# Layer 1's causal attention regrouped: four heads and half of the queries per unit, two heads per maximum, four heads' values together

## The chip, the cores and the metric

The kernel runs on one core of a Trainium2 chip. The metric is the device time of one execution in microseconds (us). A core has five engines that run their own instruction streams in order and meet at semaphores: PE (TensorE, matmuls; PEld is its weight load), DVE (VectorE), ACT (ScalarE), POOL (GpSimd) and SP (SyncE, which here only issues DMAs). Matmul results land in PSUM, eight banks of 128 partitions x 512 f32.

## The reference, cut to what matters

Two transformer layers on 1024 tokens of 256 values, each with attention, a mixture of experts, and a modulated layer norm ahead of each. The change is in layer 1's attention alone. There, 16 heads of 16 values attend causally, with a linear bias per head on the key's position (ALiBi):

```python
q = h @ Wq + bq; k = h @ Wk + bk; v = h @ Wv + bv        # h: 1024 x 256, 16 heads of 16
s = (q_h @ k_h.T) / 4 + slope_h * (key - query)          # key <= query only
o_h = softmax(s) @ v_h
x = x + gate * (concat(o_h) @ Wo + bo)
```

## The kernel before

**What a head's work is.** Queries and keys are cut into bf16 parts that are stacked on the contraction axis (`qst`, `kst`: 107 rows), so one bf16 matmul gives scores of f32 quality. For one head and one half of the queries (512 of 1024) the kernel makes:

- maxima: scores with queries on the partitions, per block of 128 queries (`j` 0 to 3) and 512 keys (`kh`), as wide as the causal mask leaves them (128, 256, 384 or 512 keys), a mask matmul on the diagonal block, and a DVE reduction to one maximum per query (`pe_max16`, `dve_max16`, L1216 to L1226);
- the row: the negated maxima go as two bf16 parts into rows 99 to 106 of `qst`, so that the next scores come out with the maximum taken off: three small DVE operations (`dve_neg`), a PE transpose into bank 6 (`pe_tr`, L1004) and a DVE product with a 0/1 mask over 11 x 512 (`dve_row16`, L1008);
- score tiles: the transposed scores, 128 keys x up to 512 queries (`pe_st16`, L1242, mask L1245), exponentiated by ACT into `Pb` (`act_exp16`, L1258);
- values: `vx` (16 values and a column of ones per head) against `Pb`, an f32 matmul with 17 output rows. Four key blocks of one head go to four 32-row strips of one bank (4 or 5), side by side (`pe_pv16`, L1279);
- the end: ACT copies the bank to `OTa` (`act_ot16`, L1291), four f32 matmuls with `esum` add the strips and transpose (`pe_evac16`, L1299), DVE divides by the sum and writes `octx` (`dve_evac16`, L1308, L1310).

**Tiling and order.** A unit is one head and one half: 32 units, head by head, the halves in turn. The first half has 4 key blocks, the second 8. `causal_order` writes one list that all engines follow; maxima run two units ahead of the score tiles. Maxima rotate over banks 0, 1 and 7, score tiles over banks 2 and 3, `Pb` over 9 buffers. `OTa` has one buffer per half.

**The stacks.** SP writes projected parts to DRAM (`sp_scratch`) and loads them back stacked (`sp_stack`), in three groups: heads 0 to 3, 4 to 7 and 8 to 15 (`GROUPS`), each group's loads behind the one before on one queue. `pe_max16` waits for the group of its head on `stacked[g]`.

**Layer 0's stage of the same shape.** Layer 0's pattern attention (`pattern_order`) already runs units of four heads and half of the queries: `pe_maxp` makes two heads' scores into a pair of banks ("slot", two slots: banks 0 and 1, 2 and 3), `dve_maxp` reduces both at once (L1074, 1024 values), `pe_shift` with `mc` and `act_shift` bring the maxima to `qst2`, score tiles rotate over banks 4, 5 and 7, `pe_pvp` puts four heads in the four strips of bank 6, `pe_evacp` does four heads at once through a slot (L1166). It has no causal mask, and its stacks have 64 rows, so two heads' score matmuls can run on PE together.

Of the kernel before, what the change touches and what calls it, by code (L numbers as in the profile page):

```python
# [15 lines left out]
H = 16  # L16
# [9 lines left out]
GROUP_OF = [0] * 4 + [1] * 4 + [2] * 8  # L26
# [7 lines left out]
LOADS2 = (((0, 0, 2), (48, 0, 1)), ((0, 0, 2), (48, 1, 1)))  # L34

# [10 lines left out]
def max_steps(nh, half, causal):  # L46

    out = []
    for a in range(nh):
        for j in range(4):  # L50
            keys = (4 * half + j + 1) * 128 if causal else T
            for kh in range(2):
                c = min(512, keys - 512 * kh)
                if c > 0:
                    out.append((a, j, kh, c))
    return out


def attention_order(nu, nh, causal, group, ahead, lag, at_begin, at_step, evac, lead=True):

    order, due, n = [], [], 0

    def steps_of(u):
        return [("max", u, *s) for s in max_steps(nh, u % 2, causal)]
# [11 lines left out]
    if lead:  # L76
        order += steps_of(0)
    neg, row = unit_head(0)
    order += neg + row
    if ahead == 2:  # L80
        order += steps_of(1)
    for u in range(nu):
        nk = (4 * (u % 2) + 4 if causal else NT) * nh
        todo = steps_of(u + ahead) if u + ahead < nu else []
        total, given = len(todo), 0
        begin, last_max = (0, nk) if ahead == 2 else (3 * (u % 2), nk - 5)
        order += at_begin(u)
        ready = []
        for k in range(nk):
# [7 lines left out]
            if ahead == 1:  # L97
                for _ in range(due_now // 2):
                    order.append(todo.pop(0))
                    due_now -= 1  # L100
# [8 lines left out]
            if len(ready) == group * nh:  # L109
# [14 lines left out]
def main_order():  # L124
# [19 lines left out]
    order = attention_order(16, 2, False, 2, 1, (2, 3, -4, -2), at_begin, at_step, evac, lead=False)  # L144
# [5 lines left out]
def pattern_order():  # L150
# [27 lines left out]
    first = [("mmax", *s) for s in max_steps(2, 0, False)]  # L178
# [59 lines left out]
def program(nc, a, out):  # L238
# [42 lines left out]
    esum = sb("esum", [128, 17], F32)  # L281
# [144 lines left out]
    octx = sb("octx", [128, NT, D], F32, at=F.at)  # L426
# [102 lines left out]
    def dve_stats(e, n, half):  # L529
        hs = slice(4 * half, 4 * half + 4)  # L530
        for j in range(4):
            i = 4 * half + j
            if n < 2:
                if j == 0 and n == 0:
                    e.wait_ge(d_x[half], 16)
                elif j == 0:
                    e.wait_ge(b6_ok[2], B6M["project", 14 + half, 1] + 1)
                e.bn_stats(st6[:, i, :], x[:, i, :]).then_inc(st_ok, 1)
# [180 lines left out]
    def sp_rows(e, l, g):  # L719
        hs = slice(*GROUPS[g])  # L720
        for st, n in ((qst, "qrow"), (kst, f"krow{l}")):
# [201 lines left out]
    NO_M, NO_C = numbered(MAIN), numbered(CAUSAL)  # L923
# [24 lines left out]
    def last_max(order):  # L948

        out, n = {}, 0  # L950
        for s in order:
            if s[0] == "max":
                n += 1
                out[s[1]] = n
        return out

# [10 lines left out]
    def bank6_table(order, kinds):  # L967

        out, n = {}, 0
        for s in order:  # L970
# [5 lines left out]


    mx_mm, mp_ok, neg_ok, tr_mm, b6_ok, st_mm, exp_ok, pv_mm, ot_ok, neg_v = (
        [s, s, sem(f"{n}m")] for n, s in ((n, sem(f"{n}16")) for n in (
            "mx_mm", "mp_ok", "neg_ok", "tr_mm", "b6_ok", "st_mm", "exp_ok", "pv_mm", "ot_ok", "neg_v")))  # L980
    ev_mm, ev_v, clear_ok, mcat_one = ([s, s] for s in (sem(n) for n in ("ev_mm", "ev_v", "clear_ok", "mcat_one")))
    ST_MM0 = EXP_OK0 = (0, 256, 0)
    NEG_OK0, OT_OK0, PV_MM0, EV_V0 = (0, 16, 0), (0, 8, 0), (0, 64, 0), (0, 16, 0)
    CLEAR_OK0 = (0, 1, 0)

    def dve_neg(e, i, u, nh, two, last):

        dst, low = mcat[:, u % 2, 0:nh, 3:7], mcat[:, u % 2, 0:nh, 7:11]
        e.wait_ge(mp_ok[i], last)
        if two:  # L990
            e.tensor_reduce(dst, mp[:, u % 3, 0:nh, :, :], AX, ALU.max, negate=True).then_inc(neg_v[i], 1)
        else:
            e.tensor_scalar(dst, mp[:, u % 3, 0:nh, :, 0], -1.0, None, ALU.mult).then_inc(neg_v[i], 1)
        e.wait_ge(neg_v[i], 2 * u + 1)
        e.tensor_copy(mbf[:, 0:nh, :], dst).then_inc(neg_v[i], 1)
        e.wait_ge(neg_v[i], 2 * u + 2)
        e.tensor_tensor(low, dst, mbf[:, 0:nh, :], ALU.subtract).then_inc(neg_ok[i], 1)

    def pe_tr(e, i, u, nh, before):
        e.wait_ge(neg_ok[i], NEG_OK0[i] + u + 1)  # L1000
        if before:
            e.wait_ge(b6_ok[i], before)
        for h in range(nh):
            last = e.transpose(bank[6][0:11, 128 * h:128 * h + 128], mcat[:, u % 2, h, :], idf[:])  # L1004
        last.then_inc(tr_mm[i], 1)
# [15 lines left out]
    RING, TILEP, BANK_P0, SHIFT = {}, {}, {}, {}  # L1021
    ring_free, slot_, turn_ = [None, None], 1, 0
    tile_free = {4: (lat_ok, LAT_ALL), 5: (lat_ok, LAT_ALL), 7: (fold_ok, 6)}
    for s_ in PATTERN:
        if s_[0] in ("max", "evac"):
            slot_ = 1 if s_[0] == "evac" and s_[1] >= 6 else 1 - slot_
            RING[s_] = (len(RING), slot_, ring_free[slot_])
            ring_free[slot_] = (ring_ok, len(RING))
        elif s_[0] == "shift" and s_[1] < 2:
            slot_ = 1 - slot_  # L1030
            SHIFT[s_[1]] = (2 * slot_, ring_free[slot_])
            ring_free[slot_] = (sh_ok, s_[1] + 1)
        elif s_[0] in ("shift", "st"):
            for a_ in range(2 if s_[0] == "st" else 1):
                b_ = (4, 5, 7)[turn_ % 3]
                turn_ += 1
                if s_[0] == "st":
                    TILEP[s_[1:] + (a_,)] = (len(TILEP), b_, tile_free[b_])
                    tile_free[b_] = (exp_ok[0], len(TILEP))
                else:  # L1040
                    SHIFT[s_[1]] = (b_, tile_free[b_])
                    tile_free[b_] = (sh_ok, s_[1] + 1)
        elif s_[0] == "product" and s_[2] == 0:
            b_ = (4, 5, 7)[turn_ % 3]
            turn_ += 1
            BANK_P0[s_[1]] = (b_, tile_free[b_])
            tile_free[b_] = (pc_ok, s_[1] + 1)
    NPBP = 11

    def pe_ring(e, s):  # L1050

        _, slot, free = RING[s]
# [4 lines left out]
    def pe_maxp(e, s):  # L1057
        _, w, j, kh = s
        hp, qi = w // 4 * 2 + w % 2, w // 2 % 2 * 4 + j
# [3 lines left out]
        slot = pe_ring(e, s)  # L1063
        for a in range(2):
            r = slice(64 * a, 64 * a + 64)
            last = e.matmul(wide[slot][:, a, :], qst2[r, hp, qi * 128:qi * 128 + 128], kst2[r, hp, cols(kh)],  # L1066
                            start=True, stop=True)
        last.then_inc(ring_mm, 1)

    def dve_maxp(e, s):  # L1070
        _, w, j, kh = s
        r, slot, _ = RING[s]
# [3 lines left out]
    def dve_negp(e, w):  # L1076

        n, m = nm[:, w % 2, :].rearrange("p (a j) -> p j a", a=2), mc[w % 2][:].rearrange("p j (a c) -> p j a c", a=2)
        e.wait_ge(ring_ok, RING["max", w, 3, 1][0] + 1)
        e.tensor_reduce(nm[:, w % 2, :].rearrange("p (a j) -> p a j", a=2), mp[:, w % 3, :, :, :], AX, ALU.max,  # L1080
# [70 lines left out]
    def act_otp(e, s):  # L1151
        _, u, kt = s
        if kt != NT - 1:
            return
# [1766 lines left out]
```

## Time and profile before

| | us |
|---|---|
| median of 3 runs | 1561.76 (1561.07 to 1561.95) |
| the profiled execution | 1559.81, of it span 1558.0 |

| engine | busy us | share |
|---|---|---|
| PE | 1423.2 | 91% |
| DVE | 924.2 | 59% |
| ACT | 746.3 | 48% |
| POOL | 548.4 | 35% |

The stage that the change touches runs from 1160.5 us (its first score matmul) to 1349.3 us (the first matmul of the output projection), 188.8 us or 12% of the span. Matmul records overlap: a record's own length is longer than the step from its start to the next one's, so PE's cost is read from the distance of starts, not from the sum of lengths. A f32 matmul leaves two records ("x8" is four matmuls).

### The profile page before, as it was taken

Reading aid. Unit: us, or ns where it says so; the run is one execution under the profiler, and the core shown is the slowest. Engines: PE = TensorE matmul, PEld = TensorE weight load, DVE = VectorE, ACT = ScalarE, POOL = GpSimd, SP = SyncE. Lnnn points to the kernel's source line nnn. Section 1 sums busy time; section 2 is a strip of 40 time slices with the busy share of each in tenths; the row PEclk is TensorE's granted clock in tenths of the full one; section 3 lists DMA queues with packets and bytes.
Section 4 is the critical chain, followed back from the end, with each engine's and each line's share of the span. In section 5 each row is a group of like instructions: output and inputs, shape, how many; then the busy total and the mean of one; then the engine's idle time right before and its main releaser. Section 6 shows DMA issues by size and latency. Waiting matters only on the chain. (4 is left out here: it accounts for less than half of the span.)

```text
span 1558.0 us, 20601 instructions
## 1 busy us (share of the span) xinstructions
PE 1423.2 (91%) x7350; PEld 837.9 (54%) x7350; DVE 924.2 (59%) x1719; ACT 746.3 (48%) x1368; POOL 548.4 (35%) x454
## 2 busy tenths in 40 slices
PE   6889999899999999999999968899689999779998
PEld 3533333355555545454555546788544444468887
DVE  5598776356566666666666343444458787534445
ACT  3468776654445454545454334233135555435553
POOL 4260152055565656556565531233300000101210
PEclk9999999999999999999999978899789999959999
DMA  7660000000000000000001011111064000101110
GB/s 291 162 135 1 6 16 8 1 1 0 1 1 0 1 1 1 1 1 1 1 1 42 1 40 36 41 41 41 1 181 81 1 1 1 51 21 41 43 40 28
DMA packets 19050, 53.03 MB, mean 34 GB/s; under 512 B 4198, under 2 KB 7032, under 8 KB 17667
## 3 DMA queue, kind: packets, MB, share of 16 engines
q1 hardware_dynamic: 18949, 51.72, 11.7%
q8 instruction: 59, 0.97, 0.3%
q14 instruction: 42, 0.34, 0.1%
HBM read 42.28 MB, written 8.39 MB: 33 GB/s over the span
## 5 line engine op out<-in xcount | busy, mean ns | idle before, releaser
L1643 POOL TENSOR_TENSOR Ps<-Ps,Pb 128x512 f32<-128x512 f32 x192 | 245.2, 1292 | 161.5 <-ACT Pb L1626 161.5
L1626 ACT ACTIVATE Pb<-bank 128x512 f32<-128x512 f32 x256 | 152.7, 597 | 288.2 <-PE bank L1615 287.7
L1587 DVE TENSOR_REDUCE mp<-bank 128x1 f32<-128x512 f32 x256 | 171.6, 686 | 143.4 <-PE bank L1580 141.4
L1074 DVE TENSOR_REDUCE mp<-bank 128x2 f32<-128x1024 f32 x128 | 153.1, 1221 | 45.4 <-PE bank L1066 45.2
L1133 ACT ACTIVATE Pb<-bank 128x512 f32<-128x512 f32 x256 | 133.3, 601 | 40.6 <-PE bank L1116 40.2
L1580 PE MATMUL bank<-qk1h,qk0h 128*128 128x512 f32 x256 | 136.0, 543 | 7.6 <-DVE mp L1587 7.6
L1612 PE MATMUL bank<-qk0h,qk1h 128*128 128x512 f32 x256 | 124.3, 486 | 6.1 <-DVE mrow L1008 6.1
L1657 PE MATMUL bank<-Pb,kvx 128*64 128x512 f32 x512 | 124.0, 605 | 0.7 <-ACT Pb L1626 0.7
L1258 ACT ACTIVATE Pb<-bank 128x512 f32<-128x512 f32 x192 | 84.7, 489 | 78.1 <-PE bank L1245 55.3
L1226 DVE TENSOR_REDUCE mp<-bank 128x1 f32<-128x512 f32 (+1 forms) x192 | 97.5, 550 | 13.7 <-PE bank L1216 11.5
L1614 PE MATMUL bank<-qk0h,qk1l 128*128 128x512 f32 x256 | 101.3, 396 | 0.0
L1613 PE MATMUL bank<-qk0l,qk1h 128*128 128x512 f32 x256 | 101.0, 394 | 0.0
L1615 PE MATMUL bank<-mrow,onesr 128*128 128x512 bf16 x256 | 100.1, 391 | 0.0
L1116 PE MATMUL bank<-qstr,kstr 64*128 64x512 f32 x256 | 87.9, 488 | 6.8 <-ACT Pb L1133 6.6
L2019 POOL TENSOR_TENSOR hl<-hf,hh 128x512 fp32r<-128x512 f32 x32 | 41.3, 1290 | 143.2 <-ACT hh L2006 143.2
L1822 POOL TENSOR_TENSOR cTt<-cTt,gab 128x256 f32<-128x256 f32 x8 | 6.5, 810 | 229.0 <-DVE cTt L1812 229.0
L1116 PEld LDWEIGHTS bank<-qstr,kstr 64*128 64x128 f32 x256 | 36.0, 185 | 86.3 <-ACT Pb L1133 58.2
L2286 POOL TENSOR_TENSOR v1l<-wr,v1h 128x512 fp32r<-128x512 f32 x25 | 32.0, 1282 | 140.6 <-ACT v1h L2281 140.6
L1643 POOL TENSOR_TENSOR Ps<-Pb,Pb 128x512 f32<-128x512 f32 x32 | 40.6, 1281 | 115.2 <-ACT Pb L1626 115.1
L1612 PEld LDWEIGHTS bank<-qk0h,qk1h 128*128 128x128 f32 x256 | 48.5, 189 | 53.7 <-issue 33.6
L1580 PEld LDWEIGHTS bank<-qk1h,qk0h 128*128 128x128 f32 x256 | 50.0, 195 | 47.6 <-DVE mp L1587 25.0
L1721 DVE SCALAR_TENSOR_TENSOR x<-bank,rcp,x 128x256 f32<-128x256 f32 x128 | 53.0, 476 | 33.1 <-PE bank L1706 33.1
(341 smaller groups left out, 3280.3 us busy)
## 6 DMA issues: line engine op xcount, KB each, us to landing
wr<-wf SPq DMA_DIRECT2D x25, 256.0 KB, 2.6
wraw<-wf SPq DMA_DIRECT2D x8, 768.0 KB, 4.1
scratch<-stgr SPq DMA_DIRECT2D x4, 1024.0 KB, 4.0
scratch<-stg SPq DMA_DIRECT2D x4, 768.0 KB, 6.2
owT<-owT SPq DMA_DIRECT2D x1, 2048.0 KB, 9.8
qbn<-qbn SPq DMA_DIRECT2D x1, 1536.0 KB, 14.9
qstr<-scratch SPq DMA_DIRECT2D x6, 256.0 KB
kstr<-scratch SPq DMA_DIRECT2D x6, 256.0 KB
```

The costliest lines, as they stand in the source:

```text
L1074: e.tensor_reduce(mp[:, w % 3, :, j, kh], wide[slot][:], AX, ALU.max).then_inc(ring_ok, 1)
L1116: e.matmul(bank[b][:], kst2[r, hp, kt * 128:kt * 128 + 128], qst2[r, hp, cols(u % 2)], start=True, stop=True).then_inc(st_mm[0], 1)
L1133: e.activation(Pbp[n % NPBP][:], bank[b][:], ACT.Exp, scale=0.25).then_inc(exp_ok[0], 1)
L1580: e.matmul(bank[b][:, 0:c], qh[:, qi * 128:(qi + 1) * 128], kh_[:, kh * 512:kh * 512 + c], start=True, stop=True).then_inc(mx_mm[2], 1)
L1587: e.tensor_reduce(mp[:, u % 3, hd, j, kh:kh + 1], bank[b][:, 0:c], AX, ALU.max).then_inc(mp_ok[2], 1)
L1612: e.matmul(o, kh[:, ks], qh[:, qs], start=True, stop=False)
L1613: e.matmul(o, kh[:, ks], ql[:, qs], start=False, stop=False)
L1614: e.matmul(o, kl[:, ks], qh[:, qs], start=False, stop=False)
L1615: e.matmul(o, onesr[:], mrow[u % 2 * 2 + hd][:], start=False, stop=True).then_inc(st_mm[2], 1)
L1626: e.activation(Pbm[n % NPBM][:], bank[b][:], ACT.Exp, scale=SC0).then_inc(exp_ok[2], 1)
L1643: e.tensor_tensor(Ps[z][:], first, Pbm[n % NPBM][:], ALU.add).then_inc(sum_ok, 1)
L1657: last = e.matmul(bank[b][64 * hd:64 * hd + 64, :], kvx[:, kt, :], Pbm[n % NPBM][:], start=(kt < 1), stop=(kt == NT - 1), skip_group_check ...
```

## The change

- **Units** are four heads (a quad) and one half: 8 units. The order is now half by half: units 0 to 3 are the first half of quads 0 to 3, units 4 to 7 the second half.
- **Maxima** are made for two heads into a slot of two banks (`pe_maxc`) and reduced together (`dve_maxc`): 96 reductions where there were 192. Widths and masks stay. The score matmuls are the same in number and width, still one head each.
- **The row** is replaced by layer 0's way: `dve_negc` (four small DVE operations per unit), `pe_shift` (four matmuls with `mc`, through one of banks 4, 5, 7 or a slot), and `act_shiftc`: two ACT copies per unit, 11 rows x 2 heads x 512. A 0/1 pattern in `kst` (`krow`) picks each head's rows. DVE's masked product is gone.
- **Score tiles** rotate over banks 4, 5 and 7 and over 18 `Pb` buffers.
- **Values** of four heads and the same key block stand in the four strips of bank 6; two key blocks are done in one go (`pe_pvp` with l = 1).
- **The end** is per unit of four heads: one copy of bank 6, one set of four matmuls, a reciprocal and a product: 8 where there were 32.
- Waits for the stacks stay on `stacked[g]`, now asked for in the order quad 0 (group 0), quad 1 (group 1), quad 2 and 3 (group 2), within the first half's units. What SP issues, and in which order, stays (but for one small constant less at the start, `esum`).
- POOL clears and presets `mc` for layer 1 (`pool_mc(e, 1)`).

```diff
+def pair_half(l, w):
+    quad, half = (w // 4, w // 2 % 2) if l == 0 else (w // 2 % 4, w // 8)
+    return 2 * quad + w % 2, half
...
 def causal_order():
-    def at_step(u, k):
-        return [("clear",)] if (u, k) == (0, 0) else []
-    return attention_order(32, 1, True, 4, 2, (2, 2, 0, 2), lambda u: [], at_step, lambda u: [(0, [("evac", u)])])
+    lead, steps = 12, [(2 * u, pr, kt) for u in range(8) for kt in range(pair_keys(1, 2 * u)) for pr in range(2)]
+    maxima = [("max", w, j, kh) for w in range(16) for j, kh in pair_max(1, w)]
+    order, behind, done = [], [], 0
+    def one_max():
+        order.append(maxima.pop(0))
+        w, n = order[-1][1], len(pair_max(1, order[-1][1]))
+        left = sum(m[1] == w for m in maxima)
+        if left == 0 and w % 2:
+            order.append(("neg", w // 2))
+        if left == n - 2 and w and w % 2 == 0:
+            order.append(("shift", w // 2 - 1))
+    for n in range(lead):
+        one_max()
+        done += 1
+    for s, (w, pr, kt) in enumerate(steps):
+        order.append(("st", w // 2, pr, kt))
+        if s == 1:
+            order.append(("clear",))
+        while maxima and done < lead + s + 1 + min(s, 32) // 4:
+            one_max()
+            done += 1
+            if not maxima:
+                order.append(("shift", 7))
+        if pr == 1 and kt % 2:
+            behind.append((s + 3, ("pv", w // 2, kt)))
+            if kt == pair_keys(1, w) - 1:
+                behind.append((s + 6, ("evac", w // 2)))
+        order.extend(b[1] for b in behind if b[0] == s)
...
+    def pe_maxc(e, s):
+        _, w, j, kh = s
+        hp, half = pair_half(1, w)
+        q0, k0, c = 512 * half + 128 * j, 512 * kh, 512 if kh < half else 128 * j + 128
+        if (j, kh) == (0, 0):
+            e.wait_ge(stacked[min(hp // 2, 2)], STACKED2 + STACKED)
+        slot = pe_ring(e, 1, s)
+        for a in range(2):
+            h = 2 * hp + a
+            last = e.matmul(wide[slot][:, a, 0:c], qst[0:99, h, q0:q0 + 128], kst[0:99, h, k0:k0 + c], start=True, stop=True)
+        if kh == half:
+            for a in range(2):
+                last = e.matmul(wide[slot][:, a, c - 128:c], idb[:], maskq[:], start=False, stop=True, skip_group_check=True)
+        last.then_inc(ring_mm, 1)
...
+        e.tensor_reduce(mpc[:, w // 2 % 3, a0:a0 + 2, j, kh], wide[slot][:, :, 0:c], AX, ALU.max).then_inc(ring_ok, 1)
...
+        for pr in range(2):
+            h = 2 * (hp + pr)
+            e.activation(qst[96:107, h:h + 2, cols(half)], bank[b][96:107, :].unsqueeze(1).to_broadcast([11, 2, 512]),
+                         ACT.Copy).then_inc(sh_ok, 1)
...
+        for t in kts:
+            c = tile_queries(l, half, t)[1]
+            for a in range(4):
+                hp = pair_half(l, 2 * u + a // 2)[0]
+                h, i = 2 * hp + a % 2, TILEP[l][u, a // 2, t, a % 2][0] - TILE0[l]
+                last = e.matmul(bank[6][32 * a:32 * a + 17, 512 - c:512], vx[:, t, h * 17:h * 17 + 17],
+                                PBR[l][i % len(PBR[l])][:, 0:c],
+                                start=(t == 0), stop=(t == pair_keys(l, 2 * u) - 1), skip_group_check=True)
```

In this order a step is one `("st", ...)`: the two score tiles of two heads for one key block. There are 96 steps, 8 per unit in the first half and 16 in the second. Twelve maxima come ahead of the first step, then 1.25 per step up to step 32 and one per step up to step 75; steps 76 to 95 have none.

## Rows read from the trace of the kernel before

**Rows 1.** Windows of the stage: engines' busy us (instructions), granted clock, DMA share, GB/s.
```profile
1160.50:1170.50 10.00, 7.67 (x38) 3.58 (x38) 8.83 (x24) 1.75 (x4) 0.00 (x0) 0.66 1.10 211
...
1160.50:1349.30 188.80, 175.32 (x1313) 88.13 (x1314) 145.43 (x387) 100.61 (x224) 0.00 (x0) 0.98 0.14 28
```
**Rows 2.** Groups by form, 1160.5 to 1349.3: busy us, mean ns of one | idle before.
```profile
L1226 DVE TENSOR_REDUCE mp<-bank 128x1 f32<-128x512 f32 x96 | 64.5, 685 | 12.9 <-PE bank L1216 11.5
...
L1279 PE MATMUL bank<-Pb,vx 128*17 128x512 f32 x192 | 49.9, 598 | 0.5 <-ACT Pb L1258 0.5
...
L1008 DVE TENSOR_TENSOR qst<-bank,dmask 11x512 bf16<-11x512 f32 x32 | 21.9, 684 | 9.2 <-PE bank L1004 7.2
...
L1242 PEld LDWEIGHTS bank<-qst,kst 107*128 107x128 bf16 x192 | 21.3, 111 | 48.2 <-ACT Pb L1258 39.3 <-issue 4.4 <-DVE qst L1008 1.2
...
L1291 ACT ACTIVATE OTa<-bank 128x512 f32<-128x512 f32 x32 | 19.1, 597 | 16.4 <-PE bank L1279 16.3
...
L1226 DVE TENSOR_REDUCE mp<-bank 128x1 f32<-128x256 f32 x32 | 13.2, 411 | 0.0
...
L1279 PE MATMUL bank<-Pb,vx 128*17 128x128 f32 x64 | 12.6, 278 | 0.0
...
L995 DVE CAST mbf<-mcat 128x4 bf16<-128x4 f32 x32 | 5.4, 170 | 1.1
```
**Rows 3.** Timeline of PE inside the stage: start us, length us.
```profile
1229.97 0.38 PE L1216 MATMUL bank<-kst,qst 99*128 99x512 bf16 x1
1230.19 0.38 PE L1242 MATMUL bank<-qst,kst 107*128 107x512 bf16 x1
...
1231.00 1.23 PE L1299 MATMUL bank<-esum,OTa 32*128 32x17 f32 x8 [0.26 <-DVE qst L1008]
1232.08 0.38 PE L1242 MATMUL bank<-qst,kst 107*128 107x512 bf16 x1
...
1233.11 1.05 PE L1279 MATMUL bank<-Pb,vx 128*17 128x512 f32 x8
1234.09 0.28 PE L1242 MATMUL bank<-qst,kst 107*128 107x256 bf16 x1
```
**Rows 4.** Timeline of layer 0's stage of four heads, same columns.
```profile
235.63 1.05 PE L1147 MATMUL bank<-Pb,vx 128*17 128x512 f32 x8
...
238.46 1.05 PE L1147 MATMUL bank<-Pb,vx 128*17 128x512 f32 x8
...
240.10 0.66 PE L1097 MATMUL bank<-idr,mc 128*128 128x128 f32 x4
```
**Rows 5.** Reductions of 1024 values in layer 0: ns min/median/max, first and last start.
```profile
L1074 DVE TENSOR_REDUCE mp<-bank x128: 1159/1225/1229, 54.5 to 266.6; 128x2 f32<-128x1024 f32 x128
```
**Rows 6.** ACT on 1024 columns, elsewhere in the kernel, same columns.
```profile
L1950 ACT ACTIVATE wh<-wraw x8: 1040/1048/1048, 910.0 to 1077.2; 128x1024 fp32r<-128x1024 f32 x8
```
**Rows 7.** Timeline: SP's issues of the third group's stacks, ACT's back-to-back tiles.
```profile
1161.46 1.25 SPq L732 DMA_DIRECT2D qst<-scratch  x3
1162.75 1.81 SPq L732 DMA_DIRECT2D kst<-scratch  x4
...
1171.76 1.08 ACT L1258 ACTIVATE Pb<-bank 128x512 f32<-128x512 f32 x2 [1.31 <-PE bank L1242]
```
**Rows 8.** Windows of the loads' end, columns as in Rows 1.
```profile
1168.00:1187.70 19.70, 17.99 (x129) 9.40 (x127) 16.52 (x45) 10.79 (x24) 0.00 (x0) 0.94 0.85 163
1187.70:1195.00 7.30, 7.05 (x62) 3.48 (x64) 6.01 (x17) 4.00 (x11) 0.00 (x0) 1.00 0.00 1
```
**Rows 9.** Layer 0's stage near its end, without maxima: timeline.
```profile
298.46 1.05 PE L1147 MATMUL bank<-Pb,vx 128*17 128x512 f32 x8
...
301.05 1.05 PE L1147 MATMUL bank<-Pb,vx 128*17 128x512 f32 x8
```
**Rows 10.** Window of that end, columns as in Rows 1.
```profile
270.00:304.00 34.00, 32.91 (x166) 10.99 (x169) 11.84 (x19) 23.84 (x46) 6.07 (x6) 0.96 0.00 1
```
**Rows 11.** All of layer 0's stage: its score tiles' first and last start.
```profile
L1116 PE MATMUL bank<-qstr,kstr x256: 383/496/793, 88.2 to 302.0; 64*128 64x512 f32 x128
```

More of the change, by code:

```diff
@@ L43, in numbered, with max_steps, attention_order @@
     return number
[L46 to L61, printed above, removed]
+def max_steps():
+    return [(a, j, kh, 512) for a in range(2) for j in range(4) for kh in range(2)]
+def attention_order(lag, at_begin, at_step, evac):
+    order, due, n, nu, nh, nk = [], [], 0, 16, 2, 2 * NT
     def steps_of(u):
-        return [("max", u, *s) for s in max_steps(nh, u % 2, causal)]
+        return [("max", u, *s) for s in max_steps()]
     def run_due():
@@ L96, in attention_order @@
             given += due_now
[L97 to L100, printed above, removed]
+            for _ in range(due_now // 2):
+                order.append(todo.pop(0))
+                due_now -= 1
             order.append(("st", u, a, kt))
@@ L720, in sp_rows @@
         hs = slice(*GROUPS[g])
-        for st, n in ((qst, "qrow"), (kst, f"krow{l}")):
+        for st, n in ((qst, "qrow"), (kst, "krow")):
             e.dma_start(st[96:107, hs, :], a[n][:, hs, :]).then_inc(stacked[g], 16)
@@ L984, in program @@
[L984 to L997, printed above, removed]
@@ L1001, in pe_tr @@
+    def pe_tr(e, u, before):
+        e.wait_ge(neg_ok[1], u + 1)
         if before:
-            e.wait_ge(b6_ok[i], before)
-        for h in range(nh):
+            e.wait_ge(b6_ok, before)
+        for h in range(2):
             last = e.transpose(bank[6][0:11, 128 * h:128 * h + 128], mcat[:, u % 2, h, :], idf[:])
-        last.then_inc(tr_mm[i], 1)
+        last.then_inc(tr_mm, 1)
     def masked_row(e, o, h):
@@ L1020, in program @@
         "ring_mm", "ring_ok", "sh_mm", "sh_ok", "nm_ok", "mc_ok", "pc_ok", "d_sw", "half_ok"))
[L1021 to L1034, printed above, removed]
+    mh_ok = sem("mh_ok")
@@ new lines, in act_shiftc, with pe_stc @@
+    def act_shiftc(e, u):
+        b, _ = SHIFT[1][u]
+        hp, half = pair_half(1, 2 * u)
+        e.wait_ge(sh_mm, 16 + u + 1)
+        for pr in range(2):
+            h = 2 * (hp + pr)
+            e.activation(qst[96:107, h:h + 2, cols(half)], bank[b][96:107, :].unsqueeze(1).to_broadcast([11, 2, 512]),
+                         ACT.Copy).then_inc(sh_ok, 1)
+    def pe_stc(e, s):
+        _, u, pr, kt = s
+        hp, half = pair_half(1, 2 * u + pr)
+        q0, c = tile_queries(1, half, kt)
+        if kt == 0:
+            e.wait_ge(sh_ok, 16 + 2 * u + pr + 1)
+        for a in range(2):
+            _, b, free = TILEP[1][u, pr, kt, a]
+            h = 2 * hp + a
+            e.wait_ge(*free)
+            last = e.matmul(bank[b][:, 0:c], kst[0:107, h, kt * 128:kt * 128 + 128], qst[0:107, h, q0:q0 + c],
+                            start=True, stop=True)
+            if kt >= 4 * half:
+                last = e.matmul(bank[b][:, 0:128], idb[:], maskk[:], start=False, stop=True, skip_group_check=True)
+            last.then_inc(st_mm[0], 1)
@@ L1140, in pe_pvp @@
             else:
[L1141 to L1148 removed]
+                e.wait_ge(clear_ok, l + 1)
@@ L1283, in act_ot16 @@
-    def act_ot16(e, s):
-        _, u, ready = s
-        half = u % 2
-        if ready[-1][1] != 4 * half + 3:
-            return
-        e.wait_ge(pv_mm[1], PV_MM0[1] + NO_C[s])
-        if u >= 2:
-            e.wait_ge(ev_mm[1], u - 1)
-        e.activation(OTa[half][:], bank[4 + half][:], ACT.Copy).then_inc(ot_ok[1], 1)
-    def pe_evac16(e, u):
-        half = u % 2
-        e.wait_ge(ot_ok[1], OT_OK0[1] + u + 1)
-        e.wait_ge(b6_ok[1], B6C["evac", u])
-        for j in range(4):
-            rows = 32 * (j + 1) if half == 0 else 128
-            last = e.matmul(bank[6][:, 128 + 17 * j:145 + 17 * j], OTa[half][0:rows, 128 * j:128 * j + 128],
-                            esum[0:rows, :], start=True, stop=True)
-        last.then_inc(ev_mm[1], 1)
```

514 lines of the change are left out of this document (242 added, 272 removed).

## The prediction

> **What bounds the kernel now.** I read the page first: PE is busy 91% of the span, no other engine above 59%. Then the windows. The stage that changes takes 188.8 us; in it PE's records cover 175 us, DVE's 145 and ACT's 101, at nearly full granted clock, 2.4 GHz, but for the first 10 us [rows 1]. So PE's queue sets this stage too. Last, the stage's groups and timeline, for what PE's time is made of. Records overlap, so I count the distance of starts: 0.22 us for a score matmul of 512 columns (so about 0.055 per 128), 0.98 us for four value matmuls of 512 to 128 columns side by side, 1.08 us for the four matmuls that end a unit [rows 3]. A mask matmul of 128 columns I take at 0.06 us. Four matmuls in four strips run together: that is why 0.98 and not a sum stands there.
>
> PE's sum before: maxima 73,728 columns and 128 masks, 31.4 + 7.7 = 39.1 us; score tiles the same, 39.1; values 48 groups of four at 0.97, 46.6; ends 32 x 1.0 = 32; transposes 32 x 0.11 = 3.5. Together 160 us of 188.8. The other 29 us are a slow start of 10 us, where PE waits for DVE at a clock of 0.66 [rows 1], the wait for DVE's row product ahead of each end, some 0.26 us [rows 3], and score tiles that wait for one of two banks (39.3 us before PE's weight loads for ACT, partly under running matmuls [rows 2]).
>
> **The change, part by part.**
>
> *Ends.* 32 sets of four matmuls become 8. A set for four heads has 68 output columns instead of 17; I take the same 1.0 us, since the 128-column weight loads set it. PE: -24.
>
> *Row.* 32 transposes (3.5 us) become 8 shifts at about 0.6 each (a record of four is 0.66 long, part of it overlaps [rows 4]): +1.3. On DVE 32 products of 684 ns [rows 2] go, -21.9 us; of the small operations of 0.17 [rows 2], 96 become 32, -10. ACT gains 16 copies of 1024 columns at about 1.05 [rows 6], +16.8, and loses 24 of the 32 copies of 0.597 [rows 2], -14.3.
>
> *Maxima.* PE the same 39.1. DVE: 685 ns for 512 values, 411 for 256 [rows 2], 1225 for 1024 [rows 5]: slope about 1.05 ns per value. 48 x 1.225 + 16 x (0.95 + 0.685 + 0.41) = 91.5 us against 104.3: -13.
>
> *Values.* Before, a group of four strips lasts as long as its widest, 0.97, whatever the others. Now the four strips are equally wide. A record of 512 columns takes 598 ns, one of 128 takes 278 [rows 2], 107 ns per 128 columns and pass, two passes; so I estimate 0.97, 0.76, 0.55 and 0.33 us for 512 to 128. The narrowest bound is proportional (0.24), the widest that nothing shrinks (0.97). Sum: 16 groups of full width 15.5, 8 times the four widths 8 x 2.61 = 20.9, together 36.4 against 46.6: -10 (between -11.6 and 0).
>
> *PE after:* 39.1 + 39.1 + 36.4 + 8 + 4.8 = 127.4 us, -33. DVE has some 103 us, ACT 83 us of tiles (two of 512 take 1.08 back to back [rows 7]) + 4.8 + 16.8 = 104. So PE still binds, but by less. Were the idle time the same 29 us, the stage would gain 33. It isn't, for two reasons.
>
> *The loads.* This is a cost that the diff does not show. The order is now half by half, so heads 8 to 15 are asked for at the seventeenth maximum, right behind step 4. Before, they were asked for half way through. Their seven stack loads, 3072 KB, are issued from 1161.5 on [rows 7], and the queue moves 163 GB/s until 1187.7, then 1 [rows 8]. 19.7 us x 163 is 3.2 MB, about that group's size, so the third group lands at about 1187.7 and the second at about 1168. Nothing that SP does is changed, so this stays. What can run before: DVE's first eight maxima from 1160.9, 2 x (0.41 + 0.69 + 0.95 + 1.22) = 6.5 us; negation 0.8; then the two maxima that need the second group, the shift and ACT's copy, so the first score tile at about 1171. Steps 0 to 4 are ten tiles at ACT's pace and one more copy: until about 1176. Then PE stands in its queue before the maximum until 1187.7, 11 to 12 us, and everything behind it with it. This hides nothing. By then the clock will be down, and the first few microseconds after it are slow; I take 2.5 us (before, the same stage began at 0.66 [rows 1]).
>
> *After 1187.7.* PE's work per stretch: steps 5 to 15, 16 us; steps 15 to 32 (1.25 maxima each, narrow tiles), 1.43 x 17 = 24.3; steps 32 to 75, 0.41 scores + 0.41 maxima + 0.41 values + 0.10 ends and shifts = 1.33 x 43 = 57.2. How much of its time PE works, I take from layer 0's stage of this form: two steps took 2.83 us, from one set of values to the next [rows 4], and hold 0.98 + 2 x 0.35 + 2 x 0.43 = 2.54 us of work, 90%. With 0.91: 107 us. Steps 75 to 95 have no maxima and go at the pace of ACT with three banks. In layer 0 two such steps took 2.59 us [rows 9]. Unit 7: five key blocks of full width 13, then 2.3, 1.8 and 1.3 for the narrower tiles, about in proportion; the rest of unit 6 about 4; the end (values, copy, matmuls, division) 3.3: 26 us.
>
> Sum: 1187.7 + 107 + 2.5 + 26 = 1323.2, against 1349.3: **-26 us**. The profiled execution's span would go from 1558.0 to 1532, its time from 1559.8 to 1533.8; the median of runs lies 2 us above that execution: 1561.8 - 26 = **1536**. POOL's memsets of `mc` and the dropped constant cost nothing: POOL stands idle over this whole stage [rows 1]. What follows is the same code, 26 us earlier, and its loads are issued at the end of this stage as before.
>
> **A rule against it.** In layer 0's last 34 us without maxima PE is busy 32.9 and the clock granted is 0.96 [rows 10], so I leave the tail at 2.4 GHz. The Trainium skill (TensorE: Matmul & The Clock Gate, section "HAM oscillation — how this bites in real kernels") says that repeated waits of PE for something else put its clock back to half, again and again. By that rule a tail paced by ACT would run half as fast on PE; the trace so far speaks against it.
>
> **The rivals.**
>
> 1. *The loads don't bite* (they land sooner than I read, or the queue is shorter because something shifts). Then the 11.5 us wait and its slow clock are not paid: -26 - 12 = -38, 1524. Against it: DMA moves data until 1187.7 [rows 8]. 10%.
> 2. *The pace of all of layer 0's stage.* There 128 steps took 302 - 88.2 = 213.8 us, 1.67 each [rows 11], with full widths and other work between. 91 steps at 1.67 from 1187.7, and 3.3 for the end: 1343, -6: 1556. For it: three banks for tiles and shifts, and values that now hold PE 1.96 us at a time, more than the 1.6 that ACT has in three banks. Against: the causal steps are narrower. 9%.
> 3. *Clock.* PE waits for ACT in every step of the tail, and the clock goes to its lower level there, as it did at the stage's start [rows 1]. The tail's 18 us of PE work at 1.2 GHz take 36 instead of 26 us: 1546. 6%.
> 4. *Slower: the turn from unit to unit is exposed.* Only 3 to 5 steps lie between a unit's last maximum and its first tile. If nothing covers the chain, each of the 7 turns costs the last reduction 1.2, negation 0.7, shift 0.6, both copies 2.1 and a tile 0.2: 4.8 us, 34 in all on top of my sum: +8, 1570. It decides from 26 / 7 = 3.7 us exposed per turn. For it: one bank of three is held by the shift while ACT copies. Against: three steps are 4 us of PE work, which cover most of the chain. 6%.
>
> **How the numbers follow.** My forecast has 69%: 1525 to 1549, from PE 96% busy instead of 91 (-6), a shorter tail (-4), to 88% (+4) and value groups that don't narrow (+10 in part, since steps paced by ACT hide some). The range for 8 in 10 adds most of rivals 1 and 2: 1519 to 1556. Faster by over 0.2% (3 us; less than that can't be told from no change): all but rival 4 and the far end of rival 2, 0.92. Same 0.03, slower 0.05.
>
> **What would show it.** The loads: one wait of PE of about 11 us before a maximum, ending at about 1187.7 on the loads of `qst` and `kst`, with the clock at 0.5 behind it. The ends: 8 sets of four matmuls of about 1.0 us with 68 columns. Values: groups of equal width at 0.97, 0.76, 0.55, 0.33 between starts. DVE's busy time in the stage 145 down to about 103; ACT's 101 up by some 2. The tail: 21 steps without maxima in about 26 us. The prediction is wrong if maxima of heads 8 to 15 start well before 1187, if turns cost over 2 us each, or if the steps in the middle take other than about 1.46 us.

## The result, and the profile after

| | before | changed |
|---|---|---|
| median | 1561.41 us | 1553.3 us |
| runs, from to | 1560.22 to 1561.95 | 1550.02 to 1554.4 |
| profiled run, span | 1559.8, 1558.0 | 1552.52, 1550.7 |

The ratio is 0.9946, with a 95% interval of 0.9928 to 0.9963: faster, by 8 us or half a percent. I had forecast a gain of 26 us, 1536. The time lies inside the range of 8 in 10 (1519 to 1556), near its upper end; the size was wrong by a factor of three.

The page of the changed kernel, its first lines:

```profile
span 1550.7 us, 19820 instructions
PE 1398.0 (90%) x7158; PEld 822.2 (53%) x7158; DVE 879.7 (57%) x1477; ACT 745.6 (48%) x1360; POOL 549.9 (35%) x458
```

Line numbers are now those of the changed kernel: L1160 the maxima's matmuls (L1163 their mask), L1172 DVE's maximum, L1139 the shift, L1197 ACT's copy of it, L1210 the score tiles (L1213 their mask), L1255 ACT's Exp, L1275 the values, L1295 the end.

**A measure that leaves layer 0 out.** The code ahead of the stage is the same in all kernels here (but for one small constant that the kernel before loads), and yet it ended anywhere between 1132.2 and 1139.6 us. So I measure a *stretch*: from ACT's first copy of layer 1's projections to PE's first matmul of the output projection. These two rows are its ends in the changed kernel, from the timelines of ACT and PE (start, length):

```profile
1137.49 0.69 ACT L681 ACTIVATE stg<-bank,bcol 128x512 bf16<-128x512 f32 x1 [1.48 <-PE bank L667]
1340.91 1.01 PE L1793 MATMUL bank<-idf,octx 128*128 128x128 f32 x6 [0.81 <-DVE octx L1314]
```

Their distance is 203.4 us. Before, the same two events lie at 1134.29 and 1349.24, distance 214.95. The stretch became 11.5 us shorter; my sum had 26 us there. That gap of 14.5 us is what the experiments are about. Of the 11.5, the profiled run kept 7.3: 3.2 us went ahead of the stretch, where the code is the same, and 1.0 behind it, where the clock was low for the first microseconds of the output projection.

The stage by windows, first the changed kernel (busy us and instructions of PE, PEld, DVE, ACT, POOL, then granted clock, DMA share, GB/s). It begins at the first maximum; the cuts are the first score tile, the end of the third group's wait, step 15, step 32, step 75, step 80 and the end:

```profile
1161.60:1178.10 16.50, 8.35 (x53) 5.05 (x52) 9.20 (x16) 3.00 (x3) 0.00 (x0) 0.68 1.04 215
1178.10:1191.05 12.95, 5.49 (x40) 3.38 (x37) 5.62 (x10) 4.87 (x11) 0.00 (x0) 0.76 0.76 157
1191.05:1213.00 21.95, 20.62 (x160) 11.77 (x160) 11.91 (x20) 11.47 (x25) 0.00 (x0) 0.76 0.01 2
1213.00:1242.80 29.80, 25.76 (x225) 13.59 (x221) 21.81 (x32) 16.93 (x40) 0.00 (x0) 1.00 0.00 1
1242.80:1308.30 65.50, 60.84 (x465) 26.88 (x463) 47.45 (x59) 44.71 (x94) 0.00 (x0) 1.00 0.00 1
1308.30:1318.40 10.10, 6.32 (x48) 2.67 (x45) 1.85 (x5) 4.49 (x10) 0.00 (x0) 0.83 0.00 0
1318.40:1340.90 22.50, 18.92 (x148) 7.05 (x145) 1.36 (x4) 15.11 (x36) 0.00 (x0) 1.00 0.01 1
sum 179.30, PE 146.31 PEld 70.39 DVE 99.21 ACT 100.59 POOL 0.00; mean PE 20.90 PEld 10.06 DVE 14.17 ACT 14.37 POOL 0.00
```

Against [rows 1]: PE's busy time went from 175.3 to 146.3, DVE's from 145.4 to 99.2, ACT's stayed at 100.6. The work did go. But 33 us of the 179 are idle on PE, 16 of them in the first two windows.

The timeline of PE shows the idle time in three kinds of places (start, length, then the wait ahead of it and what ended it). First the loads:

```profile
1172.75 0.40 PE L1160 MATMUL bank<-kst,qst 99*128 99x128 bf16 x2 [5.29 <-DMA kst<-scratch]
...
1191.05 0.39 PE L1160 MATMUL bank<-kst,qst 99*128 99x128 bf16 x2 [7.46 <-DMA kst<-scratch]
```

Second, a pair of value sets, with ACT and DVE beside it (a timeline of all engines, other PE rows left out):

```profile
1282.61 1.05 PE L1275 MATMUL bank<-Pbc,vx 128*17 128x512 f32 x8
1283.47 1.04 PE L1275 MATMUL bank<-Pb,vx 128*17 128x512 f32 x8
...
1284.88 2.37 ACT L1255 ACTIVATE Pbc<-bank 128x384 f32<-128x384 f32 x6 [1.85 <-PE bank L1213]
...
1285.65 1.23 DVE L1172 TENSOR_REDUCE mpc<-bank 128x2 f32<-128x1024 f32 x1 [1.65 <-PE bank L1163]
```

The two sets hold PE's queue from 1282.61 to 1284.45. Meanwhile ACT and DVE empty what they have: ACT then stands for 1.85 us, DVE for 1.65. After that PE waits in turn. All of the 4.7 us of idle time that its records leave between steps 32 and 75 ends on DVE, which frees a slot or has the negated maxima ready late: 2.5 us ahead of three ends, 1.4 ahead of maxima, 0.8 ahead of shifts. First a line of the waits (us, times, longest), then one of the three on PE's timeline:

```profile
PE bank L1295 <- DVE mpc L1172: 2.5, 3, 0.8
```
```profile
1275.07 1.08 PE L1295 MATMUL bank<-esum,OTa 128*128 128x68 f32 x8 [0.82 <-DVE mpc L1172]
```

Third, the last turn from one unit to the next, at steps 75 and 76, PE again:

```profile
1309.22 0.28 PE L1163 MATMUL bank<-maskq,idb 128*128 128x128 bf16 x2
1311.61 0.66 PE L1139 MATMUL bank<-idr,mc 128*128 128x128 f32 x4 [2.12 <-DVE mc L1189]
...
1314.30 0.39 PE L1210 MATMUL bank<-qst,kst 107*128 107x256 bf16 x1 [1.66 <-ACT qst L1197]
```

The shift is placed straight behind the last maximum. PE waits for the reduction and the negation (2.12 us), and then for ACT's copies (1.66 us).

### The profile page after: what moved, and what is told of

The parts are those of the page before. It is cut to its first block and busy times, and to the rows that moved or that the text cites. A ratio compares the mean times of both kernels' runs of the same rounds, so it can differ in the third digit from the quotient of the medians.

```text
span 1550.7 us, 19820 instructions
## 1 busy us (share of the span) xinstructions
PE 1398.0 (90%) x7158; PEld 822.2 (53%) x7158; DVE 879.7 (57%) x1477; ACT 745.6 (48%) x1360; POOL 549.9 (35%) x458
## 3 DMA queue, kind: packets, MB, share of 16 engines
q1 hardware_dynamic: 18805, 51.72, 11.5%
## 5 line engine op out<-in xcount | busy, mean ns | idle before, releaser
L1639 ACT ACTIVATE Pb<-bank 128x512 f32<-128x512 f32 x256 | 152.8, 597 | 288.0 <-PE bank L1628 287.6
L1255 ACT ACTIVATE Pb<-bank 128x512 f32<-128x512 f32 (+3 forms) x355 | 175.9, 575 | 61.8 <-PE bank L1230 43.1
L1172 DVE TENSOR_REDUCE mpc<-bank 128x2 f32<-128x1024 f32 (+2 forms) x96 | 88.7, 955 | 46.5 <-PE bank L1163 38.4
L1275 PE MATMUL bank<-Pb,vx 128*17 128x512 f32 (+3 forms) x710 | 97.5, 602 | 0.6 <-ACT Pbc L1255 0.4
L1230 PE MATMUL bank<-qstr,kstr 64*128 64x512 f32 x256 | 91.2, 509 | 6.7 <-ACT Pb L1255 6.2
L1230 PEld LDWEIGHTS bank<-qstr,kstr 64*128 64x128 f32 x256 | 37.6, 193 | 88.3 <-ACT Pb L1255 57.2
L1656 POOL TENSOR_TENSOR Ps<-Pb,Pb 128x512 f32<-128x512 f32 x32 | 40.7, 1284 | 116.2 <-ACT Pb L1639 116.1
L1106 PE MATMUL bank<-kstr,qstr 64*128 64x512 f32 x256 | 71.9, 459 | 1.4 <-DVE mp L1114 1.4
```

What stands on the lines that cost most here:

```text
L1172: e.tensor_reduce(mpc[:, w // 2 % 3, a0:a0 + 2, j, kh], wide[slot][:, :, 0:c], AX, ALU.max).then_inc(ring_ok, 1)
L1230: e.matmul(bank[b][:], kst2[r, hp, kt * 128:kt * 128 + 128], qst2[r, hp, cols(half)], start=True, stop=True).then_inc(st_mm[0], 1)
L1255: e.activation(PBR[l][i % len(PBR[l])][:, 0:c], bank[b][:, 0:c], ACT.Exp, scale=0.25).then_inc(exp_ok[0], 1)
L1275: last = e.matmul(bank[6][32 * a:32 * a + 17, 512 - c:512], vx[:, t, h * 17:h * 17 + 17], PBR[l][i % len(PBR[l])][:, 0:c], start=(t == 0), ...
L1639: e.activation(Pbm[n % NPBM][:], bank[b][:], ACT.Exp, scale=SC0).then_inc(exp_ok[1], 1)
L1656: e.tensor_tensor(Ps[z][:], first, Pbm[n % NPBM][:], ALU.add).then_inc(sum_ok, 1)
```

## The experiments

Four theories were on the table. The load wait: PE stands for heads 8 to 15, and the clock behind it is low. The value pairs: two sets in one go starve ACT and DVE. The last turn: nothing stands between the last maximum and its shift. And chance: that the kernel before itself varies by several us. "Stretch" below is the measure defined above, from the profiled run.

| kernel | stretch | median, ratio [95%] |
|---|---|---|
| before | 214.95 | |
| before once more | 214.97 | 1564.41, 1.0017 [1.0, 1.0034] |
| changed | 203.42 | 1553.3, 0.9946 [0.9928, 0.9963] |
| heads in another order (quads) | 204.48 | 1545.64, 0.9905 [0.988, 0.9931] |
| other data, no third wait | 196.72 | 1541.9, 0.9864 [0.9843, 0.9886] |
| values singly | 193.80 | 1541.53, 0.9858 [0.9835, 0.9882] |
| last shift later | 200.21 | 1545.64, 0.9893 [0.9874, 0.9912] |
| singly and later | 191.33 | 1536.7, 0.9837 [0.981, 0.9863] |
| the same, other data | 184.40 | 1534.11, 0.9818 [0.9787, 0.9849] |
| the same, table ahead | 190.93 | 1536.31, 0.9833 [0.981, 0.9855] |
| the same, other order | 181.66 | 1527.93, 0.977 [0.9752, 0.9788] |
| the same, order and table | 183.76 | 1528.91, 0.9785 [0.9757, 0.9813] |

The medians scatter by more than the stretches do: the changed kernel's own median, 1553.3, has a stretch 3.2 us longer than "last shift later" and a median 7.7 us longer. Where the two differ I go by the stretch, and by the medians for whether a version is faster at all. The parts of the stretch behind step 15 repeat far better than the whole. Steps 32 to 75 take 65.6 us in each of the three kernels with paired values in the changed kernel's order, and 62.4 us in each of the four with single ones; steps 15 to 32 take 29.8 and 29.1.

**Before, once more.** The unchanged kernel of before ran as an experiment, against itself.

> The kernel before once more, for a second profile of it. Ahead of the stage the changed kernel's profile is 3.2 us late, with TensorE's clock low for 23.9 us in layer 0 (82 to 106 us) where the first profile of before shows 3.4 us. If that is chance, this profile's stage may start 1 to 5 us later than in the first; if it belongs to the change, it starts within 0.5 us of it.

The stretch was the same to 0.02 us, though the clock was low for 23.9 us of layer 0's stage (60 to 330 us) instead of 10.2. The missing 14.5 us are far more than either difference between these two profiles. The medians of this one kernel, 1564.41 here and 1560.3 beside it, lie 4 us apart. The stretch began 0.9 us later than in the first profile, between the two values expected. That the changed kernel's began 3.2 us late is not of the change all the same: three kernels below with its code ahead of the stretch began at 1132.2 to 1133.5 us, earlier than before's 1134.3, each with 10.2 us of low clock in layer 0; the changed kernel had 34.1 there. In windows of 60 to 330 us (layer 0's stage), before and before once more:

```profile
60.00:330.00 270.00, 248.42 (x1326) 102.14 (x1325) 194.03 (x241) 177.69 (x333) 79.49 (x70) 0.98 0.13 33
```
```profile
60.00:330.00 270.00, 248.87 (x1307) 102.44 (x1308) 192.75 (x238) 177.57 (x333) 79.51 (x70) 0.96 0.12 29
```

The mean granted clock is 0.98 in one and 0.96 in the other, for the same instructions; the changed kernel had 0.94 there, with code that it shares with before.

**Heads in another order.** Both halves of quads 0 and 1 first, then quads 2 and 3, so that heads 8 to 15 are needed half way through:

```diff
-quad, half = (w // 4, w // 2 % 2) if l == 0 else (w // 2 % 4, w // 8)
+quad, half = (w // 4, w // 2 % 2) if l == 0 else (w // 2 % 2 + 2 * (w // 8), w // 4 % 2)
...
-while maxima and done < lead + s + 1 + min(s, 32) // 4:
+while maxima and done < lead + s + 1 + min(5 * s // 8, 10):
```

> The changed kernel with its units in another order: quads 0 and 1, first half then second half, then quads 2 and 3 the same way. The third group of stacks (heads 8 to 15) is then asked for at maximum 48 of 96, not 16; the maxima run a little further ahead (ten more than the steps, not eight), since the first long unit now comes early. Theory A (the order's wait for the third group, 7.5 us in the trace after, and the low clock of 13.7 us behind it are a main part of what the prediction missed): that wait is gone and the clock is up from about 1185 us on, so 10 to 14 us less than the changed kernel: 1539 to 1543 us. Theory B (that wait only covers DVE's maxima and ACT's tiles that would be late anyway): within 3 us of 1553.

The wait for the third group was gone, and the stretch of the profiled execution was no shorter. Step 5 came 3.0 us behind step 4 instead of 9.9, and the part behind step 75 was 5.9 us shorter; but steps 5 to 48 took 80.8 us instead of 74.8, and 48 to 75, which now hold two short units with their turns, 47.4 instead of 40.6. The clock was low in five places behind the second group's wait, 27 us together instead of 17 in two. That execution was the slowest of this kernel's five, 1555.0 us; the others took 1545.2 to 1550.1, and the median, 1545.64, is 7.7 us below the changed kernel's, between the two theories. So its stretch can't stand for the kernel, and the run moves several things at once: it doesn't price the wait. The next one does.

**Other data, no third wait.** The first half of quads 2 and 3 uses the stacks of quads 0 and 1, which are there already; same order, same instructions. The kernel leaves out the first half's own scores of heads 8 to 15. The replacement in the last two lines is made in `pe_maxc`, `act_shiftc` and `pe_stc`.

```diff
+def stack_pair(w):
+    hp, half = pair_half(1, w)
+    return (hp if half else hp % 4), half
...
-        hp, half = pair_half(1, w)
+        hp, half = stack_pair(w)
```

> The changed kernel, order and widths untouched, but in the first half the units of quads 2 and 3 read (and write the maxima's rows into) the stacks of quads 0 and 1, so they don't wait for the third group before unit 6's first maximum. It leaves out the first half's scores of heads 8 to 15, whose output is other heads' instead. It takes the third group's wait away and nothing else. Theory A: 7.5 us of wait and some 3 us of low clock gone: about 1543. Theory B: 1551 to 1553, the time comes back in the waits of DVE and ACT.

The stretch lost 6.7 us and the median came to 1541.9, near theory A's 1543. The wait itself was 7.46 us, so nearly all of it was on the path, and little of the low clock went with it: the 5.3 us wait for the second group stayed, and brought its own.

**Values singly.** The values of each key block stand by themselves instead of two blocks together:

```diff
-        if pr == 1 and kt % 2:
+        if pr == 1:
             behind.append((s + 3, ("pv", w // 2, kt)))
...
-        kts = ((kt,), (kt - 1, kt))[l]
+        kts = (kt,)
```

> The changed kernel with values one key block at a time, as in layer 0, instead of two. Theory C (1.9 us of values in one go outlast the 1.6 us that three banks of tiles give ACT, so ACT runs dry and PE then waits for it): the middle steps fall from 1.53 to about 1.47 us and the tail from 32.6 by some 3: 1547. Theory D (PE's work binds, the grouping only moves the waits): 1552 to 1554.

9.6 us of stretch and 11.8 of the median, more than either theory gave. The middle, steps 32 to 75, is the clean place. The window of this kernel that answers to 1242.80:1308.30 above:

```profile
1239.40:1301.80 62.40, 61.54 (x464) 25.54 (x464) 47.52 (x59) 45.47 (x95) 0.00 (x0) 1.00 0.00 1
```

It is 3.1 us shorter, with the same number of matmuls; PE's idle time fell from 4.7 to 0.9 us, and none of it ends on DVE any more. Theory C's forecast, 0.06 us a step here (2.6 in all) and some 3 in the tail, is about what came; what it didn't have is the part ahead of step 32. Its mechanism is half right: the long hold does leave ACT dry, but PE's own waits that went were those for DVE. The edit halves the hold and also issues the first set of each pair two steps earlier, and no run separates the two. The rest of the 9.6: 3.3 us between the wait's end and step 15, 0.7 from there to step 32, 2.4 behind step 75. In the first of these the clock takes part: behind the third group's wait it was back at 2.4 GHz 10.5 us after the release in the changed kernel (9.6 with the last shift later), but 4.9 us after it here (3.8 and 5.4 in two of the kernels below that also take values singly). Five kernels agree on this, though none moves the clock alone. A single set between score tiles, of this kernel's timeline:

```profile
1266.09 0.41 PE L1275 MATMUL bank<-Pb,vx 128*17 128x128 f32 x8
1266.43 0.11 PEld L1210 LDWEIGHTS bank<-qst,kst 107*128 107x128 bf16 x2 [0.21 <-ACT Pbc L1255]
```

**Last shift later.** The last unit's shift two steps further back; nothing else.

```diff
             if not maxima:
-                order.append(("shift", 7))
+                behind.append((s + 2, ("shift", 7)))
```

> The changed kernel with the last unit's shift two steps later (behind step 77, not right behind the last maximum at step 75). Theory E (this turn alone has no maxima between the last one and the shift, so PE stands for DVE's last reduction and negation, 2.1 us, and then for ACT's copies, 1.7 us): 2 to 3 us less: 1550.5. Rival: the copies end later by as much as the shift starts later, so the last unit's first tile waits as long: 1553.

3.2 us of stretch, 3.6 of it behind step 75 (0.4 went the other way ahead of step 15). PE's timeline at the same place:

```profile
1306.63 0.22 PE L1213 MATMUL bank<-maskk,idb 128*128 128x128 bf16 x1
1307.97 0.66 PE L1139 MATMUL bank<-idr,mc 128*128 128x128 f32 x4 [1.13 <-DVE mc L1189]
1308.48 0.23 PE L1210 MATMUL bank<-qst,kst 107*128 107x128 bf16 x1
```

Four tiles now stand between the maximum and the shift. The wait of 2.12 us is 1.13, and the second one, for the copies, is hidden by tiles that don't need them. The 3.4 us of low clock at the turn went too.

**Singly and later.** Both edits together.

> The changed kernel with values one key block at a time and the last shift two steps later. If the two causes are separate, their gains in the stretch from the first projection copy to the output projection (9.1 and 2.8 us) add up: 191.5 us there, and a time of 1538 to 1540. If both remove the same idle time, no better than values one at a time alone: 194.3 us, 1541.5.

191.33 us, where 203.4 - 9.6 - 3.2 = 190.6: the two are separate causes in the main. Only behind step 75 do they overlap: each alone takes 2.4 and 3.6 us off the 32.6 there, both together 4.6. Windows of this kernel from the wait's end, cut at the same steps:

```profile
1185.10:1204.00 18.90, 18.63 (x160) 10.75 (x160) 11.64 (x20) 11.52 (x25) 0.00 (x0) 0.86 0.01 2
1204.00:1233.10 29.10, 26.12 (x225) 13.12 (x221) 22.55 (x34) 16.78 (x39) 0.00 (x0) 1.00 0.00 1
1233.10:1295.50 62.40, 61.59 (x465) 25.52 (x466) 47.52 (x59) 45.43 (x95) 0.00 (x0) 1.00 0.01 1
1295.50:1323.50 28.00, 23.44 (x193) 9.05 (x189) 3.52 (x10) 20.21 (x46) 0.00 (x0) 1.00 0.01 1
```

PE is busy 99% in the first and third windows, so there PE's own work is the limit. Some 3 and 4.6 us are left in the second and the last.

**The same, other data.** The edit of the data on top of both.

> On top of both: the first half's units of quads 2 and 3 use the stacks of quads 0 and 1 and leave out their own scores, so the third group isn't waited for. It shows what the wait costs once the other two causes are gone. If PE's queue is what counts, the 6 us that it cost before are still there: 185 us in the stretch, 1533. If less, the tiles had been hiding it: 189, 1537.

The stretch lost another 6.9 us: 184.40, and a median of 1534.11, as expected for a wait that lies on PE's queue. The wait for the third group costs as much when the other two causes are gone as when they are there.

**The same, other order.** A version that needs no other data: quads in the order 0, 1, 0, 2, 3, 1, 2, 3 with halves 0, 0, 1, 0, 0, 1, 1, 1, so that a unit of 16 steps stands ahead of heads 8 to 15.

```diff
-... else (w // 2 % 4, w // 8)
+... else ((0, 1, 0, 2, 3, 1, 2, 3)[w // 2], (0, 0, 1, 0, 0, 1, 1, 1)[w // 2])
...
-while maxima and done < lead + s + 1 + min(s, 32) // 4:
+while maxima and done < lead + s + 1 + min(5 * s // 8, 8):
```

It was first tried with one more edit, a dummy Exp of one column on ACT ahead of the stage (the table of Exp is then loaded there):

> On top of both: units in the order quads 0, 1 (first half), 0 (second half), 2, 3 (first half), 1, 2, 3 (second half), so that the third group of stacks is asked for at maximum 32, and maxima up to 8 further ahead by step 13 already; ACT loads its exponential's table ahead of the stage. The wait for the third group should be gone, and 4 to 8 us with it: about 1534. Rival: as with quads in pairs, DVE's maxima and the turn into the first long unit take the place of the loads: 1538 to 1542.

It took 1528.91 us, 7.8 less than with both edits alone and 5 below the expected 1534. Then each part by itself, the table's load alone and the order alone:

> b1_both plus one dummy Exp on ACT ahead of the stage, so that the table of Exp is loaded (1.28 us) before the first tile instead of in front of it. The stretch from the first projection copy to the output projection was 191.33 us in b1_both. Theory E (the load of the table lies on the path of the first tiles, and everything after waits in turn): the first tile 1.3 us earlier; but PE then only stands longer in front of the seventeenth maximum, whose time the third group's loads set (released at about 1189 to 1191), so nothing of it reaches the end: stretch 191.0 to 191.6. Theory F (the steps behind the wait are relieved too): 190.0.

> b1_both plus only the order of units in which the third group's heads come later (quads 0, 1, 0, 2, 3, 1, 2, 3 with halves 0, 0, 1, 0, 0, 1, 1, 1) and the maxima's pace for it; no dummy Exp. b2_order, with both edits, had a stretch of 183.76 us, b1_both 191.33. With the third group's wait gone the first tiles are on the path to the end, so the table's load costs its 1.28 us here: 184.9 to 185.2 by theory E; by theory F the order gave 6.3 and the load of the table 1.3 in both places. If the table cost nothing anywhere: 183.8.

The order is worth 9.7 us of stretch (191.33 to 181.66), 2.8 more than taking the wait away by other data; what the new order moves besides the wait is not told apart. The table's load is worth nothing. With the table alone the stretch was near theory E's (190.93), but not for its reason: the first tile came no earlier (40.7 us into the stretch, 39.8 without). The order alone fits neither (181.66, nearest to "cost nothing anywhere"). So the load costs nothing in either place, which ACT's timeline explains, first with the load in the stage (order alone), then without it (table alone):

```profile
1174.06 1.93 ACT L1197 ACTIVATE qst<-bank 11x1024 bf16<-11x1024 f32 x2 [20.51 <-PE bank L1139]
1176.01 1.28 ACT L1255 ACT_TABLE_LOAD   x1
1177.86 1.13 ACT L1255 ACTIVATE Pb<-bank 128x512 f32<-128x512 f32 x2 [0.57 <-PE bank L1213]
```
```profile
1169.91 1.93 ACT L1198 ACTIVATE qst<-bank 11x1024 bf16<-11x1024 f32 x2 [19.24 <-PE bank L1140]
1173.71 1.13 ACT L1256 ACTIVATE Pb<-bank 128x512 f32<-128x512 f32 x2 [1.87 <-PE bank L1214]
```

The Exp starts 1.87 us behind the copies' end either way (1174.06 + 1.93 + 1.87 = 1177.86): it waits for PE's tile, and the 1.28 us of the load lie under that wait. The two kernels with the new order differ by 2.1 us of stretch: 1.0 ahead of step 5, nothing between step 5 and step 75, and 1.1 behind it, where the clock was low for 3.4 us in one of them. So I take 2 us as what a whole stretch is good for. "The same, other order" is the fastest kernel of the study, 1527.93 us (with the table ahead 1528.91, not to be told from it), 2.3% less than before; the changed kernel had 0.5%.

## Why the prediction was right or wrong

Times in the stretch, forecast (from its own instants, less 1134.29), changed kernel, and the kernel with both edits:

| part | forecast | changed | both edits |
|---|---|---|---|
| to the third group's release | 53.4 | 53.6 | 52.9 |
| release to step 15 | 20.1 | 22.0 | 18.9 |
| step 15 to 32 | 26.7 | 29.8 | 29.1 |
| step 32 to 75 | 62.9 | 65.6 | 62.4 |
| step 75 to the end | 26.0 | 32.6 | 28.0 |

1. *Loads: right.* Not in the diff, and where I had it: a wait of PE before the maximum behind step 4, ended by the DMA. The release came 53.6 us into the stretch, 53.4 forecast. It was 7.5 us long and not 11 to 12, since step 4 came later: the second group landed some 1.5 us later than I read it (PE waited 5.3 us for it), and the first tiles ran at a clock of 0.7. Nothing of that delay reached the end, the release did. Taken away, the wait for the third group gives back 6.7 to 6.9 us.
2. *Ends, row, narrow values: right.* Eight sets of four matmuls, records of 1.0 to 1.1 us; a set of 128 columns takes 0.34 between starts (0.33 forecast). DVE's 99.2 and ACT's 100.6 us stand near the forecast 103 and 103.
3. *"How much of its time PE works": the step that failed.* I took 91% from layer 0's stage and let it stand for every effect between the engines. By the forecast's own measure, work counted from starts over time, the middle is 57.2 of 65.6 us with pairs, 87%, and 57.2 of 62.4 with single sets, 92%: the 0.91 was right for single sets and wrong for pairs. The pairs of value sets cost 9.6 us in the whole stretch. Their hold stands in rival 2, with its numbers, "values that now hold PE 1.96 us at a time, more than the 1.6 that ACT has in three banks", and it was left there at 9% and not put in the sum. It can be read from [rows 3 and 4] that both stages before issue one set at a time: the row that I took 91% from held no pair. What rival 2 didn't have is who passes the delay on to PE: the idle time of PE that the records show between steps 32 and 75 all ends on DVE.
4. *PE's work: counted too low, and partly made up by item 3's ratio.* With both edits PE's records cover 61.6 us between steps 32 and 75, where I had counted 57.2, and 26.1 between 15 and 32 instead of 24.3. Records and starts are two measures: in the two steps of layer 0 that gave 90%, I counted 2.54 us of work and the records cover 2.62 of the 2.83. So part of this gap was already in the 0.91. The rest, more work than counted and less idle time (99% busy here, 93% there), cancelled: that the middle of that kernel came within 0.5 us of the forecast is partly luck.
5. *The tail: the last turn was not priced.* The tail is the largest gap of the table, 6.6 us; the last turn is 3.6 of them (3.2 in the whole stretch). Rival 4 named the chain and priced it at 4.8 us per turn, for all seven or none. It was exposed at the one turn where no maxima are left to fill it. Rival 4 as a whole didn't come: at the other turns behind the third group's wait PE stands at most 0.8 us at a time.
6. *Clock.* Behind the load wait I took 2.5 us. The clock was at 1.2 GHz (0.5) for 10.5 us after the release, and PE's records cover 10.0 of them. A full value set took 1.68 us there and 0.87 at 2.4 GHz, from start to start, so on PE alone those 10.5 us would cost about 5 (an estimate). How much of it reaches the end no run isolates: release to step 15 took 18.9 us with 5.4 us of low clock (both edits) and 18.4 with none (the same, other data). Rival 3 didn't come: from step 80 on PE waits for ACT again and again, under 1 us a time, and the clock granted is 1.00. The rule that I put beside that rival, of the Trainium skill (TensorE: Matmul & The Clock Gate, "HAM oscillation — how this bites in real kernels"), is told there of PE standing for a DMA in every pass of a loop; I had stretched it to short waits for ACT. The trace agrees with it at waits of microseconds alone: the two load waits (5.3 and 7.5 us), and the last turn's two (2.1 and 1.7 us).

Of the forecast's three signs of being wrong, the first didn't come (the release was at 53.6 us of the stretch, 53.4 forecast). The other two did: the last turn cost over 2 us, and the steps in the middle took 1.52 us each where 1.46 was forecast.

So 14.5 us are missing from the stretch: 9.6 by the pairs, 3.2 by the last turn, and 1.7 left. The 1.7 are not mere scatter. With both edits the stretch is 191.3 us where 188.9 was forecast; steps 15 to 32 are 2.4 us over and the tail 2.0 us over, the same in three kernels, and the other three parts are 2.2 us under. Between steps 15 and 32 there was more work than counted (1.8 us, item 4), and maxima follow at 1.25 per step (DVE is busy 22.6 of 29.1 us); no run moved these alone, and the tail's 2.0 us stay open. Between the stretch's 11.5 us and the median's 8.1 stand the parts around it. In the profiled execution they are 3.2 us ahead, with 34.1 us of low clock in layer 0 against 10.2, and 1.0 behind; no run controlled layer 0's clock.

## What to carry to other kernels

A share of busy time taken from another stage holds only for the order in which that stage issues; before using it, ask for each instruction that the change makes longer on the critical engine whether its neighbours' buffers last that long, and put the answer into the sum. A new order of units also changes which loaded data is asked for when: follow the loads' landing times, and place the unit that needs the last load behind the longest unit that doesn't. Where the same code ahead of the change can end several us apart, compare the distance of two events around the change as well as the medians.

## What the hardware showed that I had not expected

- The granted clock of layer 0's stage differs between runs with the same code: in windows of 60 to 330 us, 0.94 to 0.98, and the stretch then starts up to 7 us apart: at 1132.2 to 1134.3 us in the four kernels with 10.2 us of low clock there, at 1136.7 to 1139.6 in the five with 30.7 to 34.1 us.
- After a wait of 6 to 7.5 us the clock stayed at 1.2 GHz for 9.6 to 10.5 us with paired values and 3.8 to 5.4 us with single ones. PE was busy 95% of that time or more in all five. Why the two groups differ is open.
- At half the clock a value set takes twice as long: a full one 0.87 us at 2.4 GHz and 1.68 at 1.2 GHz, from its start to the next set's. Two rows of the changed kernel's PE timeline; each is two sets, the first a full one and one of 384 columns at 1.2 GHz, the second two full ones at 2.4 GHz:

```profile
1196.96 3.19 PE L1275 MATMUL bank<-Pb,vx 128*17 128x512 f32 x16
...
1306.49 1.91 PE L1275 MATMUL bank<-Pbc,vx 128*17 128x512 f32 x16
```

- ACT's copy of 11 partitions by 1024 columns takes 1008 ns, nearly as long as one of 128 partitions (1048 ns [rows 6]).
